# Logits, exponentials and pair sums in another order in the expert-key stage of a two-layer transformer kernel

## What is computed

```python
q = jnp.einsum('btd,ed->bte', hidden_states, W_q)
q = q.reshape(b, t, 2, h, n).transpose(2, 0, 1, 3, 4)          # h = 4 heads
sim = jnp.einsum('pbthn,hkpn->pbthk', q, keys)                 # 64 keys on each side
scores_xy, idx_xy = jax.lax.top_k(sim, K)                      # K = 8
...
scores, pk = jax.lax.top_k(all_scores, K)                      # 8 of the 64 sums
...
w = jax.nn.silu(jnp.einsum('btd,bthkd->bthk', hidden_states, de) * jax.nn.softmax(scores, axis=-1))
experts_states = jnp.einsum('bthk,bthkd->btd', w, ue)
dense = jnp.einsum('bti,di->btd', jax.nn.silu(jnp.einsum('btd,id->bti', hidden_states, W_up)), W_down)
return dense + experts_states
```

## Time and profile before

| | us |
|---|---|
| median of 3 runs | 1135.71 |
| lowest, highest | 1132.48, 1136.11 |
| the profiled execution | 1129.27 |
| its span | 1127.5 |
| TensorE busy in it | 1001.2 (89%) |
| VectorE busy | 783.4 (69%) |
| ScalarE busy | 652.5 (58%) |
| GpSimd busy | 497.7 (44%) |

### The profile page before, as it was taken

One profiled execution on the slowest core, in us unless ns is written; L12 is line 12 of the kernel. 1 busy time (PEld: TensorE's weight loads), 2 busy tenths in 40 slices (PEclk: granted clock), 3 DMA queues, 4 the chain that ended last, 5 costly groups with the idle time before them and its releaser, 6 DMA issues.

```text
span 1127.5 us, 17009 instructions
## 1 busy us (share of the span) xinstructions
PE 1001.2 (89%) x5550; PEld 633.1 (56%) x5550; DVE 783.4 (69%) x1755; ACT 652.5 (58%) x874; POOL 497.7 (44%) x550
## 2 busy tenths in 40 slices
PE   8789999989778989989999779899998887999991
PEld 3345444434466778778777564344443333888881
DVE  7767688887888787787787346788888845344443
ACT  3356667666566766676677434576675560555550
POOL 6458898896415434433543342115051435122220
PEclk9899999999999999999999999999999889999996
DMA  8754979648999600000002231376554328222226
GB/s 245 224 171 161 289 194 354 192 156 267 230 220 217 124 1 1 1 2 0 1 6 74 62 104 54 112 209 150 149 148 121 96 81 342 62 70 71 71 62 224
DMA packets 74201, 149.89 MB, mean 133 GB/s; under 512 B 7823, under 2 KB 44577, under 8 KB 72580
## 3 DMA queue, kind: packets, MB, share of 16 engines
q1 hardware_dynamic: 61380, 98.80, 34.0%
q0 software_dynamic: 10800, 47.63, 11.9%
q10 hardware_dynamic: 1936, 2.36, 0.6%
HBM read 73.14 MB, written 76.25 MB: 133 GB/s over the span
## 4 chain that ended last, share of the span: by engine, by line
PE 63%; DVE 14%; ACT 10%; issue 5%; DMA 3%; POOL 3%; SPq 1%; ACTq 0%; DVEq 0%; POOLq 0%
PE ps L1313 15%; PE ps L1447 10%; PE ps L1428 7%; PE ps L1413 5%; PE ps L1387 4%; PE ps L1397 3%; PE ps L1655 3%; ACT pt L1105 3%; PE ps L1618 3%; PE ps L1632 3%; DVE negmax L1852 2%; PE ps L1776 2%; PE ps L1456 2%; PE ps L1331 1%; DVE moe_w L2198 1%
## 5 line engine op out<-in xcount | busy, mean ns | idle before, releaser
L1852 DVE TENSOR_REDUCE negmax<-ps 128x2 f32<-128x1024 f32 x256 | 309.7, 1222 | 60.2 <-PE ps L1413 58.2
L1105 ACT ACTIVATE pt<-ps 128x1024 f32<-128x1024 f32 x256 | 259.2, 1027 | 137.4 <-PE ps L1428 135.6
L1447 PE MATMUL ps<-pt,v_aug 128*32 128x512 f32 x1024 | 145.4, 634 | 3.9 <-POOL pt L804 3.1
L1428 PE MATMUL ps<-sq,sk 57*128 57x512 f32 (+1 forms) x512 | 129.2, 503 | 6.8 <-DMA sq<-m_sb 3.9
L1413 PE MATMUL ps<-sk,sq 56*128 56x512 f32 (+1 forms) x512 | 108.5, 429 | 18.8 <-ACT pt L1105 15.0
L804 POOL TENSOR_TENSOR pt<-pt,near 128x256 f32<-128x256 f32 x128 | 92.5, 730 | 51.0 <-ACT pt L1105 50.4
L1428 PEld LDWEIGHTS ps<-sq,sk 57*128 57x128 f32 (+1 forms) x512 | 49.4, 190 | 109.1 <-issue 71.0
L996 POOL DMA_INDIRECT expert_out<-yo,dest x39 | 38.1, 977 | 116.4 <-ACT yo L1280 101.7
L908 POOL TENSOR_TENSOR w_first<-w_first,moe_w 128x1024 f32<-128x1024 f32 x16 | 38.1, 2380 | 104.4 <-DVE pt L2190 103.6
L1618 PE MATMUL ps<-sel,hl 128*128 128x512 f32 x256 | 72.3, 415 | 5.1 <-DVE pt L2190 5.1
L1413 PEld LDWEIGHTS ps<-sk,sq 56*128 56x128 f32 (+1 forms) x512 | 50.5, 194 | 40.5 <-ACT pt L1105 28.4
(11 more groups left out here) (323 smaller groups left out, 2059.5 us busy)
## 6 DMA issues: line engine op xcount, KB each, us to landing
expert_rows<-zero SPq DMA_DIRECT2D x3, 5586.0 KB, 61.7
expert_weights_split<-wst POOLq DMA_DIRECT2D x8, 2048.0 KB, 8.5
qk_rows<-hl SPq DMA_DIRECT2D x30, 512.0 KB, 3.1
sk<-qk_rows SPq DMA_DIRECT2D x62, 192.0 KB, 5.0
sq<-qk_rows SPq DMA_DIRECT2D x62, 192.0 KB, 4.5
moe_w<-in_w POOLq DMA_DIRECT2D x16, 512.0 KB, 7.7
wexp<-expert_weights_split POOLq DMA_DIRECT2D x16, 512.0 KB, 4.8
wexp<-expert_weights_split SPq DMA_DIRECT2D x4, 2048.0 KB, 16.7
```

What stands on the lines that cost most here:

```text
L1105: act.activation(pt[:, 4 * (U % 2) + 2 * half:4 * (U % 2) + 2 * half + 2, :], ps[:, bank:bank + 2, :], ACT.Exp, scale=(BIAS, SCALE)[L]).th ...
L1428: ins = pe.matmul(ps[:, key.bank + s, :], sk[r, pair, c * P:(c + 1) * P], sq[r, pair, :], start=True, stop=True)
L1447: ins = pe.matmul(ps[32 * j:32 * j + 32, OBANK, :], v_aug[:, b % 2, c, HG * g + j, :], pt[:, 4 * (U % 2) + j, :], start=(c == 0), stop=(c ...
L1852: dve.tensor_reduce(negmax[:, n % 2, col:col + 9:8], ps[:, job.bank:job.bank + 2, :], AX, ALU.max, negate=True).then_inc(s_jd, 1)
```

## The change

Instructions are put in another order; none is added or dropped. TensorE's `logits(s, 2)` goes between the first half of the down products and the second transpose of the weights, and `logits(s, 3)` behind the second half; both stood among the expert products. ScalarE follows: `expand(s, 2)` between the two copies of the weights, `expand(s, 3)` behind the second copy and `small_exp`, ahead of the copy of the similarities. On VectorE only `pair_sum` stays ahead of `top8`; `pair_rest` goes behind `norms8`, and `norm1` behind the first `times_hidden`. Tile 15's `first_cx(0)` stays where it was.

```diff
--- before.py
+++ after.py
@@ -1191,11 +1191,14 @@
             attention(0)
 
             act.copy(ff1s[0], wff1[:]).then_inc(s_wh, 1)
+            def weights_half(n, i):
+                if n:
+                    act.wait_ge(s_yu, n)
+                front_copy(accT[:, 512 * i:512 * i + 512], ("at", n, i))
+
             def weights_copy(n):
                 for i in range(2):
-                    if n:
-                        act.wait_ge(s_yu, n)
-                    front_copy(accT[:, 512 * i:512 * i + 512], ("at", n, i))
+                    weights_half(n, i)
 
             def row_high(kind, i):
                 front_copy(hl[:, 2 * (kind == "k") + i, 0], (kind, 0, i), ACT.Relu)
@@ -1215,16 +1218,18 @@
                     expand(s, 0)
                     expand(s, 1)
                 if s >= 3:
-                    weights_copy(s - 3)
+                    weights_half(s - 3, 0)
+                if s:
+                    expand(s, 2)
+                if s >= 3:
+                    weights_half(s - 3, 1)
                 if s:
                     small_exp(s)
-                    expand(s, 2)
+                    expand(s, 3)
                 if s + 2 < NTL:
                     sim_copy(s + 2)
                 if s == 15:
                     first_values(0)
-                if s:
-                    expand(s, 3)
                 if s % 2 and (s + 3) // 2 < NTL // 2:
                     x_high((s + 3) // 2)
                 if s in (13, 14):
@@ -1709,13 +1714,17 @@
                 if y >= 0:
                     turn_weights(y, 0)
                     ff_down(y, 0)
+                if s:
+                    logits(s, 2)
+                if y >= 0:
                     turn_weights(y, 1)
                     ff_down(y, 1)
+                if s:
+                    logits(s, 3)
+                if y >= 0:
                     add_experts(y, range(0, 3))
                 if s == 15:
                     first_values(0)
-                if s:
-                    logits(s, 2)
                 if s == 0:
                     pe.wait_ge(s_jd, at[0, "wo", B - 1, 1].done)
                 if s + 2 < NTL:
@@ -1724,8 +1733,6 @@
                     first_values(1)
                 if y >= 0:
                     add_experts(y, range(3, 6))
-                if s:
-                    logits(s, 3)
                 if s % 2 and (s + 3) // 2 < NTL // 2:
                     turn_norm((s + 3) // 2)
                 if s in (13, 14):
@@ -2257,8 +2264,9 @@
             for s in range(NTL):
                 if s >= 2:
                     turned_low(s)
+                odd_norm = s % 2 and (s + 3) // 2 < NTL // 2
                 if s % 2 and s >= 5:
-                    add_pair((s - 5) // 2)
+                    pair_sum((s - 5) // 2)
                 if s == 3:
                     dve.wait_ge(s_r1, 1)
                     stats(3 * TT, x_tok[:, 3], range(TT))
@@ -2268,8 +2276,6 @@
                     rstd2_seed(s // 13, s // 13 + 1)
                 if 2 <= s + 1 < NTL:
                     top8(s + 1)
-                if s % 2 and (s + 3) // 2 < NTL // 2:
-                    norm1((s + 3) // 2)
                 if s == 15:
                     dve.wait_ge(s_r2, 1)
                     first_cx(0)
@@ -2277,9 +2283,13 @@
                     mask(s, 0)
                     mask(s, 1)
                     times_hidden(s, 0)
+                    if odd_norm:
+                        norm1((s + 3) // 2)
                     mask(s, 2)
                     times_hidden(s, 1)
                     norms8(s)
+                    if s % 2 and s >= 5:
+                        pair_rest((s - 5) // 2)
                     mask(s, 3)
                     times_hidden(s, 2)
                 if s % 2 and (s + 3) // 2 < NTL // 2:
```

## The result

The change made the kernel faster. The first measurement gave 1120.04 us (1116.88 to 1123.03, four executions) against 1135.91 (1132.48 to 1137.04, four): a ratio of 0.9865 [0.9838, 0.9892], 15.9 us. The forecast was 6.2. Because these two did not fit, the changed kernel was measured three times more, each time beside the kernel before on one chip. The clock is TensorE's granted clock, mean over the executions.

The account below looks back on a forecast made before the run. Even tiles were taken as bound by TensorE to within 0.7 us, odd tiles by VectorE behind three GpSimd sums. -4.5 - 0.7 - 1.7 + 2.1 + 1.2 - 2.6 = -6.2 us gave a median of 1129.5, range 1119.5 to 1134.5.

Parts of the forecast that it names:

- even tiles 6, 8, 10, 12: Earlier logits and expands let VectorE end about 1.8 us sooner; TensorE's idle 0.71 and 0.17 overlap give -0.9 us each.
- even tile 4: Same gain as the other even tiles from earlier logits 2 and 3 and expand 2 and 3: -0.9 us.
- tiles 0 to 3: The norm moved into VectorE's 1.33 us idle behind `times_hidden` 0 saves 0.87 us in each of tiles 1 and 3.
- odd tiles 5, 7, 9, 11: The moved pair comes back behind the third sum with added contention, the norm's move saves 0.87: +0.53 us each, +2.1.
- tile 15: Logits 2 and 3 no longer behind expert products and next block's values; mask 3 at 630.2 instead of 632.77: -2.6 us.
- The odd tile's sum of 6.64, 12.61 and 4.28: Odd tile in us: start to mask 0, mask 0 to mask 3, mask 3 to next `hidden`; before 9.28, 9.44, 4.28.
- the clock held "as now": TensorE waits about 1 us for mask 0 and 2 us at an odd tile's end, so its clock falls as before.
- rival B: Shorter pause keeps the clock up in tiles 6, 8, 10, 12, needing c near 0: -16.0 us, 1119.7; chance 0.10.
- c: Time the pair's updates lose beside GpSimd's two `clamped_pairs` products in their new place: taken as 1.1 us, 0 to 1.37.
- rival C: Norm's second instruction locked out, third sum ends 0.7 us later, and c is 1.37: -2.1 us, 1133.6; chance 0.13.
- A: VectorE's first update gets in ahead of GpSimd in odd tiles, so c is 0.4: -10.4 us, 1125.3; chance 0.25.
- D: TensorE's pauses add up, lower clock lasts another stretch in tiles 4 to 14, 1.5 us each: +2.8, 1138.5; chance 0.10.

Follow-up runs that it names:

- logits_and_pair: Against the changed kernel, the norm put back ahead of mask 0; the logits' move and the pair behind `norms8` kept: ratio 0.9958.
- filled: `ff_up` of tiles 4, 6, 8, 10, 12 makes 12 products twice: changed kernel so edited 1118.48 us (0.9875), kernel before so edited 1129.35 us (0.9984).
- pairs_apart: Changed kernel, with GpSimd's `clamped_pairs` waiting for mask 3 in odd tiles from 5 on: 1116.09 us, ratio 0.9868.
- logits_only: Changed kernel with VectorE's moves undone; only logits 2 and 3 and expand 2 and 3 moved: 1135.53 us, ratio 1.0046.
- top8_split: Logits' move kept; in odd tiles 5 to 13 `top8` cut in four, pair and norm back in front: 1109.39 us (0.9802), again 1110.43 us (0.9775).

## Why the forecast was right and where it was wrong

Tile by tile, the mean of the four traces of after less that of two of before, beside the terms of the sum:

| term | forecast | traces |
|---|---|---|
| even tiles 6, 8, 10, 12 | -3.6 | -5.6 |
| even tile 4 | -0.9 | -0.5 |
| tile 14 | -0.7 | -0.7 |
| tiles 0 to 3 | -1.7 | -0.4 |
| odd tiles 5, 7, 9, 11 | +2.1 | +1.1 |
| tile 13 | +1.2 | +0.8 |
| tile 15 | -2.6 | -2.1 |
| stage | -6.2 | -7.4 |

**Right.** Even tiles were bound by VectorE's last product by 0.7 us and are bound by TensorE now; at the lower clock they went from 21.38 (the first trace of before) to 20.50, the 0.9 of the sum. Tile 14 is exact. The odd tile's sum of 6.64, 12.61 and 4.28 came out as 6.78, 12.29 and 4.25. The moved pair is not hidden, contends with GpSimd, and makes the odd tile longer.

**The step that failed: the clock held "as now".** The sum left the clock of tiles 6, 8, 10 and 12 where it was, since the pause ahead of them would be about as long, and rival B made a higher clock depend on c near 0. The pause was about as long, as forecast: in tile 11 it went from 1.74 to 1.59, in all four odd tiles from 1.74 to 2.06 down to 1.56 to 1.81. But the clock did not fall behind each of them: 6 of 16 such tiles in the four traces of after were at the upper clock for their `hidden`, 1 of 8 in those of before. One such tile saves 1.6 us (18.9 against 20.5). In the first trace of after there were two, and the even tiles gave 6.7 us for the 3.6 of the sum; on average they gave 5.6. Of the 2 us more, about 0.65 come from the long tile 6 of the second trace of before (22.68), the rest from the number of tiles at the upper clock. Why the clock stays up more often is open. That the 0.2 us less of pause does it is not shown, and two things speak against it: in after it was tile 6, behind the longest pause (1.80), that stayed up, 3 times of 4, and tiles 8, 10 and 12, behind 1.56 to 1.61, only 3 times of 12; and in `logits_and_pair` tiles 8, 10 and 12 were all low behind 1.49 to 1.51. With 24 tiles the two shares could also differ by chance. That the clock falls because of the pause is shown: filled, all eight tiles are at the upper clock; with pauses of 0.75 to 0.99, all four.

**The other step: one execution's time carried over to the median of a few.** I took a scatter of 0.3% from three executions. Twelve executions of one kernel differ by over 1% and follow the clock. Of the 15.9 us the stage accounts for 7.4 on average and 9.3 in the first pair of traces; the remainder, 6.6 to 8.5 us, lies in code that both kernels share. The later measurements, 0.9914 and 1.0002 among them, fit with it being the clocks that few executions happened to get; for the first one itself that is not shown, since the clocks of three of its four executions of before were not recorded. I treated the sum's basis as firm when four executions of a kernel leave its median open by several microseconds. The bound of 3.4 us for what a measurement can tell was too small as well.

**c.** Taken as 1.1, bounded by 0 and 1.37, measured 0.81 (1.69 less 0.88). As I had argued, GpSimd starts first (533.28 against 533.37). Each update then ends 0.28 us behind the end of one of its two products, so part of it overlaps; the updates lost 0.34 and 0.47 us, where the ceiling had 0.63 and 0.74. The Trainium skill (SBUF — State Buffer, "SBUF: two separate sides") has the engine that starts first keep the pair for its whole instruction; the second half of the norm, 2.52 us beside a sum and ended with it, agrees. The rows of both places fit one thing more, that two instructions issued back to back do not keep the other engine out: it got in between them.

**The norm.** Its second instruction was locked out for 2.1 us (rival C), and yet the third sum ended 8.82 us behind mask 0, as before (8.80). GpSimd lost nothing; VectorE lost time that it would have lost at `exm`. My 0.2 was too much and C's 0.7 wrong in kind. Tile 3 gave 1.05 for 0.87, but tiles 0 to 2 together came out 0.6 longer. Tiles 1 and 2 have no down products, so that logits 2 and 3 stand directly behind logits 1 and wait for mask 0; the forecast had priced that wait only in tiles with expert products. It was not tried apart, and the single traces of these tiles differ by over a microsecond.

**Tile 4.** -0.5 for -0.9: the sum took nothing for logits 2, which wait 0.98 us for mask 0 there. In tiles 6 to 12 that wait is not there, as the sum had it.

**Tile 15.** -2.1 for -2.6. Mask 3 is 12.15 behind mask 0 (forecast 12.41) and `ff_up` 3.56 behind mask 3 (before 3.59), but mask 0 itself came 6.64 behind `hidden` instead of 5.83: VectorE waits 3.06 us for ScalarE's exponentials there, 1.09 before. Tile 14 has become 0.7 shorter on TensorE and not on ScalarE, whose exponentials of tile 15 start 24.78 us behind `hidden` of tile 14 (before 24.72), and that gain was given back here. I had kept the 5.83.

**Rivals.** A (c = 0.4) is out by its own signs: the updates took 1.69 us, not under 1.4, and odd tiles 23.3, not 22.8. B's mechanism, a clock that stays up, came in part without its condition; with the condition it is what `pairs_apart` then showed. D, more stretches at the lower clock, appeared in no trace of after in tiles 4 to 14; `logits_only` is its mechanism, with a pause of 3.8 us instead of 1.15.

## What to carry to other kernels

Where TensorE is the bottleneck it pays twice for a pause: once for the pause, and once for the lower clock behind it, so price each end-of-loop pause with both, and look for the edit that shortens or fills it. Where two engines share memory, put what the other engine's chain would hold (here norms and updates with operands in SBUF alone) ahead of that chain, and fill the chain with what it does not hold (here instructions that read PSUM, and the maxima and index searches in `top8_split`). And before a small gain is believed or doubted, set the executions' clocks beside their times.

## What was not expected of the hardware

- Time follows the granted clock by 6.9 us for each 0.01, and executions of one kernel got 0.94 to 0.96 without any change of the code.
- A VectorE pair of two 128x256 instructions beside a chain of GpSimd sums took 2.84 us instead of 0.74: the first went through in 0.41, the second was held for a whole sum. The sums kept their 2.39 and 4.92 us.
- The same lock caught a 128x32 comparison (L2032 above), 1.01 us instead of 0.17, and in these traces no instruction that reads PSUM: the masks took 1.25 to 1.29 us beside the sums and without them.
- Behind a pause of 0.75 to 0.99 + 0.55 us `hidden` ran at the upper clock 4 times of 4 (`pairs_apart`), behind 1.49 to 1.51 + 0.55 in none of 3 (`logits_and_pair`), behind 1.56 to 1.81 + 0.55 in 6 of 16 (after), behind 1.74 to 2.06 + 0.55 once in 8 (before). The length of the pause alone does not order them.
